# Hybrid attention, RWKV and mixture-of-experts kernel: the steps of iterations 6 to 14 take other slots

## What is computed

```python
x = x + attention(layernorm(x))          # causal, one head, W_Q W_K W_V
x = x + moe(layernorm(x))                # 32 experts of width 64, top 4, plus a shared expert of width 128
x = x + rwkv_block(layernorm(x))         # time mixing (a recurrence over tokens), then channel mixing of width 512
x = x + moe(layernorm(x))                # the same experts again
```

## Time and profile before

| what | value |
|---|---|
| median of 3 runs | 845.95 us (844.31 to 846.03) |
| the profiled execution's own time | 845.29 us |
| its span in the trace | 843.0 us |
| mean granted clock of PE, share of full | 0.998 |
| busy share of PE, DVE, POOL, ACT | 96%, 79%, 71%, 68% |

### The profile page before, as it was taken

How to read it: one execution, slowest core, us unless ns; L and a number is a source line. 1 busy time by engine, 2 the same in 40 slices (tenths; PEclk the granted TensorE clock), 3 DMA queues, 4 the chain that set the end, 5 groups by cost and what they waited for, 6 DMA issues and landing times. The chain is left out here.

```text
span 843.0 us, 12771 instructions
## 1 busy us (share of the span) xinstructions
PE 810.1 (96%) x3876; PEld 607.2 (72%) x3876; DVE 668.9 (79%) x1539; ACT 569.4 (68%) x1033; POOL 597.8 (71%) x470
## 2 busy tenths in 40 slices
PE   7799999999999999999999999999999989999998
PEld 4577878667676676777678776787767757778785
DVE  6776777898898988989786897868977788777765
ACT  3587785877758767679474875748665675677453
POOL 2178778858767678488586876857687684967775
PEclk9999999999999999999999999999999999999999
DMA  9054443334145152550544407443264323526542
GB/s 320 18 126 104 101 97 75 83 76 104 38 103 113 42 126 50 104 126 1 132 89 116 108 16 151 103 108 81 53 136 111 83 63 69 127 50 125 117 115 72
DMA packets 47892, 80.73 MB, mean 96 GB/s; under 512 B 3280, under 2 KB 12624, under 8 KB 47440
## 3 DMA queue, kind: packets, MB, share of 16 engines
q1 hardware_dynamic: 47536, 79.72, 41.0%
q10 hardware_dynamic: 288, 0.20, 0.1%
HBM read 75.19 MB, written 4.72 MB: 95 GB/s over the span
## 5 line engine op out<-in xcount | busy, mean ns | idle before, releaser
L473 POOL TENSOR_TENSOR m_h<-m_v,m_wb 128x512 f32<-128x512 f32 x256 | 344.2, 1355 | 145.1 <-issue 47.1
L563 ACT ACTIVATE m_th<-pa 128x512 f32<-128x512 f32 x240 | 142.6, 596 | 136.4 <-PE pa L827 132.9
L1185 DVE TENSOR_TENSOR m_v<-m_th,pb 128x512 f32<-128x512 f32 x224 | 151.2, 677 | 29.0 <-PE pb L827 11.0
L336 POOL TENSOR_TENSOR m_hl<-m_h,m_hh 128x512 fp32r<-128x512 f32 x85 | 114.8, 1350 | 52.1 <-ACT m_hh L725 51.7
L825 PE MATMUL pa<-m_xh,w1h 128*128 128x512 f32 x272 | 141.7, 521 | 0.3 <-issue 0.3
L725 ACT ACTIVATE m_hh<-m_h 128x512 fp32r<-128x512 f32 x178 | 111.3, 626 | 33.1 <-POOL m_h L473 32.9
L825 PE MATMUL pb<-m_xh,w3h 128*128 128x512 f32 x272 | 117.9, 433 | 5.5 <-DVE m_v L1185 5.4
L336 DVE TENSOR_TENSOR m_hl<-m_h,m_hh 128x512 fp32r<-128x512 f32 x93 | 84.0, 904 | 41.0 <-ACT m_hh L725 41.0
L827 PE MATMUL pb<-m_xh,w3l 128*128 128x512 f32 x272 | 107.9, 397 | 0.0
L826 PE MATMUL pb<-m_xl,w3h 128*128 128x512 f32 x272 | 107.8, 396 | 0.0
L826 PE MATMUL pa<-m_xl,w1h 128*128 128x512 f32 x272 | 107.7, 396 | 0.0
(11 more groups left out here) (259 smaller groups left out, 1640.3 us busy)
## 6 DMA issues: line engine op xcount, KB each, us to landing
m_wb<-w_scratch SPq DMA_DIRECT2D x126, 512.0 KB, 6.7
x_sb<-in_x SPq DMA_DIRECT2D x8, 256.0 KB, 7.2
m_wb<-in_w SPq DMA_DIRECT2D x2, 1024.0 KB, 6.7
x_out<-x_sb SPq DMA_DIRECT2D x7, 256.0 KB, 7.0
...
```

The source lines that it names most:

```text
L336: eng.tensor_tensor(m_hl[:, at, :], hidden(g, p), m_hh[:, at, :].bitcast(F32), ALU.subtract)\
L473: pool.tensor_tensor(hidden(g, p), gated(g, p), m_wb[:, p % (GRING * GP), :], ALU.mult).then_inc(sig["m_h"], 1)
L563: ins = act.activation(m_th[:, p % 2, :], pa[p % 2][:, :], ACT.Silu)
L1185: dve.tensor_tensor(gated(g, p), m_th[:, r, :], pb[r][:, :], ALU.mult).then_inc(sig["m_v"], 1)
```

## The change

Only slot numbers change, for modes 2 to 6 (iterations 6 to 14), on all four compute engines. No operation, wait, tile, transfer or unit comes or goes, and the sets NATIVE and LOW_ON_POOL stay. In each tuple the entries of modes 0, 1 and 7 are the same as before. Lines that only "..." stands for are unchanged; each pair is one step, in the order POOL, ACT, PE, DVE.

The moves that the text below speaks of, slot before and after (the same slot number on two engines is not the same moment):

| engine, line, step | mode 3 (6, 8, 10) | mode 4 (7, 9, 11) | mode 2 (12) |
|---|---|---|---|
| PE L1030, output product of time mixing | 10 to 7 | | 11, same |
| PE L986, expert counts | 47, same | 36 to 37 | 38 to 41 |
| PE L996, transposes of r_w | 48 to 49 | 42, same | 46 to 47 |
| PE L1062, value product | 47 to 50 | 50, same | 50 to 49 |
| PE L1023, receptance | 45, same | | 33 to 37 |
| PE L976, router product | 34 to 32 | 24 to 30 | 23 to 24 |
| ACT L667, L670, exponentials | 45 to 42 | | 33 to 35 |
| ACT L663, t_r | 46 to 43 | | 36, same |
| ACT L660, t_v | 37 to 33 | | 33 to 28 |
| ACT L628, r_wT | 48 to 45 | 42 to 40 | 47 to 43 |
| DVE L1309, L1320, softmax and top 4 | 41, 41 to 34, 39 | 24, 29 to 30, 31 | 27, 36 to 27, 34 |
| DVE L1339 to L1349, r_w and r_carry | 45 to 43 | 34 to 37 | 39 to 37 |
| DVE L1391 to L1399, scans | | 1 to 2 | 44 to 43 |
| DVE L1402, L1405, denominator, numerator | | 1 to 5 | 44 to 43 |
| DVE L1465, reciprocals 0; 1; 2 and 3 | | 33; 41; 40 to 7; 23; 17 | 45; 53; 51 to 44; 51; 50 |
| POOL L498, L500 | 38 to 35 | | 28 to 25 |
| POOL L503, L505 | 39 to 37 | | 33 to 36 |
| POOL L510, input of channel mixing added | 34 to 43 | 40 to 50 | 46 to 40 |

```diff
--- before.py
+++ after.py
...
 def pro_step(q, slot, mode):
-  if slot == (0, 16, 3, 13, 7, 11, 1, 20)[mode]:
+  if slot == (0, 16, 1, 11, 11, 8, 0, 20)[mode]:
...
-  if slot == (15, 24, 17, 30, 41, 43, 37, 28)[mode]:
+  if slot == (15, 24, 17, 29, 43, 40, 36, 28)[mode]:
...
 def time_begin(m, slot, mode):
-  if slot == (3, 0, 2)[mode]:
+  if slot == (3, 1, 2)[mode]:
...
-  if slot == (17, 15, 20)[mode]:
+  if slot == (17, 16, 19)[mode]:
...
-  if slot == (30, 28, 38)[mode]:
+  if slot == (30, 25, 35)[mode]:
...
-  if slot == (33, 33, 39)[mode]:
+  if slot == (33, 36, 37)[mode]:
...
 def channel_step(m, slot, mode):
-  if slot == (46, 34, 40, 40)[mode]:
+  if slot == (40, 43, 50, 35)[mode]:
...
-  if slot == (9, 17, 19, 17)[mode]:
+  if slot == (10, 16, 18, 16)[mode]:
...
-  if slot == (22, 26, 29, 29)[mode]:
+  if slot == (23, 25, 31, 31)[mode]:
...
 def pro_step(q, slot, cmix, mode):
-  if slot == (12, 24, 17, 23, 17, 31, 11, 19)[mode]:
+  if slot == (12, 24, 14, 25, 22, 32, 13, 19)[mode]:
...
-  if slot == (17, 27, 20, 31, 19, 34, 15, 21)[mode]:
+  if slot == (17, 27, 22, 27, 26, 35, 16, 21)[mode]:
...
-  if slot == (18, 27, 26, 35, 24, 38, 19, 24)[mode]:
+  if slot == (18, 27, 26, 33, 30, 38, 19, 24)[mode]:
...
-  if slot == (35, 44, 47, 48, 42, 45, 36, 35)[mode]:
+  if slot == (35, 44, 43, 45, 40, 45, 41, 35)[mode]:
...
 def time_begin(m, slot, q, mode):
-  if slot == (16, 10, 15)[mode]:
+  if slot == (16, 10, 17)[mode]:
...
-  if slot == (19, 17, 20)[mode]:
+  if slot == (19, 16, 20)[mode]:
...
-  if slot == (28, 25, 33)[mode]:
+  if slot == (28, 24, 32)[mode]:
...
-  if slot == (35, 33, 37)[mode]:
+  if slot == (35, 28, 33)[mode]:
...
-  if slot == (37, 36, 46)[mode]:
+  if slot == (37, 36, 43)[mode]:
...
-  if slot == (36, 33, 45)[mode]:
+  if slot == (36, 35, 42)[mode]:
...
 def channel_step(m, slot, mode):
-  if slot == (38, 34, 41, 38)[mode]:
+  if slot == (38, 31, 39, 37)[mode]:
...
-  if slot == (19, 28, 27, 29)[mode]:
+  if slot == (17, 25, 27, 28)[mode]:
...
-  if slot == (28, 30, 31, 31)[mode]:
+  if slot == (28, 26, 35, 35)[mode]:
...
-  if slot == (42, 36, 43, 40)[mode]:
+  if slot == (42, 35, 43, 41)[mode]:
...
-  if slot == (42, 38, 44, 44)[mode]:
+  if slot == (42, 36, 45, 41)[mode]:
...
-  if slot == (42, 40, 47, 44)[mode]:
+  if slot == (42, 38, 45, 41)[mode]:
...
-  if slot == (42, 41, 47, 45)[mode]:
+  if slot == (42, 41, 45, 43)[mode]:
...
-  if slot == (47, 41, 47, 47)[mode]:
+  if slot == (42, 45, 46, 45)[mode]:
...
-      if slot == (10, 10, 10, 9, 8, 10, 11, 11)[it.mode]:
+      if slot == (10, 10, 9, 11, 10, 9, 11, 11)[it.mode]:
...
 def pro_step(q, slot, begin, cmix, mode):
...
-  if slot == (18, 27, 18, 29, 22, 35, 16, 9)[mode]:
+  if slot == (18, 27, 19, 29, 26, 33, 17, 9)[mode]:
...
-  if slot == (20, 29, 23, 34, 24, 38, 19, 17)[mode]:
+  if slot == (20, 29, 24, 32, 30, 37, 19, 17)[mode]:
...
-  if slot == (30, 40, 38, 47, 36, 44, 30, 22)[mode]:
+  if slot == (30, 40, 41, 47, 37, 45, 26, 22)[mode]:
...
-  if slot == (36, 44, 46, 48, 42, 45, 35, 30)[mode]:
+  if slot == (36, 44, 47, 49, 42, 47, 39, 30)[mode]:
...
 def time_begin(m, slot, q, cmix, mode):
-  if slot == (19, 17, 20)[mode]:
+  if slot == (19, 17, 19)[mode]:
...
-  if slot == (31, 24, 34)[mode]:
+  if slot == (31, 24, 32)[mode]:
...
-  if slot == (35, 30, 39)[mode]:
+  if slot == (35, 33, 34)[mode]:
...
-  if slot == (38, 33, 45)[mode]:
+  if slot == (38, 37, 45)[mode]:
...
 def time_out(m, slot, q, mode):
-  if slot == (11, 11, 10, 8)[mode]:
+  if slot == (11, 11, 7, 6)[mode]:
...
 def channel_step(m, slot, q, mode):
-  if slot == (22, 30, 33, 31)[mode]:
+  if slot == (22, 28, 34, 33)[mode]:
...
-  if slot == (43, 39, 43, 42)[mode]:
+  if slot == (45, 35, 45, 42)[mode]:
...
-  if slot == (44, 40, 45, 43)[mode]:
+  if slot == (45, 37, 46, 43)[mode]:
...
-  if slot == (45, 41, 46, 45)[mode]:
+  if slot == (46, 40, 47, 44)[mode]:
...
-  if slot == (46, 42, 47, 45)[mode]:
+  if slot == (46, 44, 47, 46)[mode]:
...
-  if slot == (50, 47, 50, 50)[mode]:
+  if slot == (49, 50, 50, 50)[mode]:
...
-      if slot == (13, 21, 15, 23, 13, 27, 14, 14)[it.mode]:
+      if slot == (13, 21, 13, 25, 12, 30, 13, 14)[it.mode]:
...
 def pro_step(q, slot, cmix, mode):
-  if slot == (1, 16, 2, 15, 5, 9, 2, 22)[mode]:
+  if slot == (1, 16, 0, 11, 10, 9, 0, 22)[mode]:
...
-  if slot == (5, 20, 10, 20, 15, 15, 4, 22)[mode]:
+  if slot == (5, 20, 7, 24, 18, 15, 7, 22)[mode]:
...
-  if slot == (16, 28, 22, 32, 24, 35, 20, 27)[mode]:
+  if slot == (16, 28, 24, 29, 28, 36, 20, 27)[mode]:
...
-  if slot == (18, 28, 27, 41, 24, 35, 20, 28)[mode]:
+  if slot == (18, 28, 27, 34, 30, 37, 20, 28)[mode]:
...
-  if slot == (19, 34, 36, 41, 29, 38, 22, 30)[mode]:
+  if slot == (19, 34, 34, 39, 31, 37, 20, 30)[mode]:
...
-  if slot == (29, 40, 39, 45, 34, 41, 30, 34)[mode]:
+  if slot == (29, 40, 37, 43, 37, 42, 32, 34)[mode]:
...
 def time_begin(m, slot, mode):
-  if slot == (4, 2, 2)[mode]:
+  if slot == (4, 1, 2)[mode]:
...
-  if slot == (10, 7, 10)[mode]:
+  if slot == (10, 7, 12)[mode]:
...
-  if slot == (27, 16, 29)[mode]:
+  if slot == (27, 17, 26)[mode]:
...
-  if slot == (29, 25, 36)[mode]:
+  if slot == (29, 27, 36)[mode]:
...
 def time_finish(m, slot, mode):
-  if slot == (42, 44, 1)[mode]:
+  if slot == (42, 43, 2)[mode]:
...
-  if slot == (44, 44, 1)[mode]:
+  if slot == (44, 43, 5)[mode]:
...
-  if slot == (46, 45, 33)[mode]:
+  if slot == (46, 44, 7)[mode]:
...
-  if slot == (50, 53, 41)[mode]:
+  if slot == (50, 51, 23)[mode]:
...
-  if slot == (49, 51, 40)[mode]:
+  if slot == (49, 50, 17)[mode]:
...
-  if slot == (51, 53, 43)[mode]:
+  if slot == (51, 53, 45)[mode]:
...
-  if slot == (53, 53, 47)[mode]:
+  if slot == (53, 53, 49)[mode]:
...
 def time_out(m, slot, mode):
-  if slot == (7, 9, 10, 13)[mode]:
+  if slot == (7, 11, 8, 10)[mode]:
...
 def channel_step(m, slot, mode):
-  if slot == (42, 34, 37, 34)[mode]:
+  if slot == (40, 28, 39, 36)[mode]:
...
-  if slot == (5, 12, 1, 12)[mode] and m == 0:
+  if slot == (5, 17, 17, 7)[mode] and m == 0:
...
-  if slot == (10, 16, 19, 16)[mode]:
+  if slot == (11, 17, 19, 16)[mode]:
...
-  if slot == (14, 24, 25, 24)[mode]:
+  if slot == (16, 20, 27, 22)[mode]:
...
-  if slot == (33, 31, 35, 31)[mode]:
+  if slot == (31, 26, 37, 33)[mode]:
...
-  if slot == (51, 51, 49, 49)[mode]:
+  if slot == (52, 53, 52, 51)[mode]:
...
-      if slot == (11, 20, 12, 23, 8, 27, 10, 10)[it.mode]:
+      if slot == (11, 20, 16, 25, 13, 29, 11, 10)[it.mode]:
```

## The result

The changed kernel takes 838.14 us (median of 4 runs, 837.64 to 840.14) beside 845.13 of the kernel before (4 runs): a ratio of 0.9922, 95% interval 0.9900 to 0.9943. The forecast was 843.8 with a range of 839.0 to 850.5, so it had the sign and a third of the size, and the time lies under the range. The profiled execution took 837.64, its span 835.9.

A forecast was written before the change was run, and what follows sets the result against it. PE's work was taken as the bound wherever it does not wait; +2.4 - 5.1 + 0 + 0.6 = -2.1 us took the profiled 845.29 to 843.2, 843.8 as median (0.66 higher), range 839.0 to 850.5.

The forecast's parts named there:

- What bounds the kernel: Whole kernel: PE's work bounds it (busy 96%), so the change is worth the PE waits it removes or makes.
- The four kinds of the prediction: PE waits, iterations 6 to 14: r_carry 3.2, DVE's gate 4.0, POOL's low part 1.0, t_v 1.9; given as 10.7 us.
- Part 1: End of iterations 6, 8, 10 (mode 3): value product uncovers a shortened chain, transposes at 48.4; +0.8 each, +2.4 us.
- The bounds: End of iterations 6, 8, 10: from -1.1 an iteration (three: -3.4) to +2.9 (three: +8.7).
- the reasons given: End of 6, 8, 10: earlier softmax, top 4 and exponentials, unit 13's low part after r_w, L510 moved, shorten the chain.
- Part 2: Starts of iterations 7, 9, 11 (mode 4): earlier m_wb and gate 1 remove PE waits; -1.7 each, -5.1 us.
- Part 3: Iterations 12 to 14: in 12 t_v's wait is replaced by a similar later one, 0; 13 and 14 together +0.6.
- A: Ends of 6, 8, 10: value product missed as cover, chain ends nearer 50.5; slower, 850.2 us; chance 0.27.
- B: Iterations 6, 8, 10: the clock falls, 1.7 us each; slower, 848.9 us; chance 0.10.
- C: All waits at the ends go; faster, 838.1 us, or 834.5 if iteration 12 loses its wait too; chance 0.13.

The follow-up runs named there:

- the test with the one entry back: Changed kernel with one entry put back, the copy t_v (L660) in mode 2 on ACT at slot 33 instead of 28: 0.9878, 835.33 us.

## Why the prediction was wrong

**What bounds the kernel**: right in kind. PE's waits in iterations 6 to 14 go from 11.4 to 5.7 us, at the places that the earlier trace rows name; that is about 5.7 of the 7.0. The rest is in the main the clock of iteration 12, 0.97 before and 1.00 here. (The four kinds of the prediction add up to 10.1, not 10.7; the 10.7 has a fifth in it, 0.6 for the normalised tile in iteration 12.)

**Part 1, the step that failed.** "I walked the new order by hand ... the high part of unit 12 (0.6), its low part on DVE beside L505 (until 46.4), gate 14 (0.7), and r_pos, r_w, r_carry (1.3): the transposes can start at 48.4". They start at 46.6. Of the 1.85, 0.63 is ACT (exponentials at 43.67, not 44.3). 0.85 is the low part: I let DVE stand behind L505, but it began 0.09 ahead and took 0.69, so it ends at 44.92; where it begins 0.06 behind, the run with softmax and top 4 back shows 1.77, the length in the earlier trace rows (the walk had left 1.5 for it). Then 0.60 from there to the end of r_carry (44.92 to 46.32, 1.40 instead of 2.0), and this is the same thing again: r_w began 0.28 ahead of POOL's next product and took 0.47. In the kernel before, it began behind one (POOL L473 at 498.61):

```profile
499.43 1.05 DVE L1343 SCALAR_TENSOR_TENSOR r_w<-r_pos,r_ws 128x128 f32<-128x128 f32 x1
```

Of all this, 0.23 is not gained, since PE had not yet come to the transposes. The rest of the part is right: from transposes to end 4.8 was forecast and 4.8 measured (51.4 - 46.6), and the value product does uncover the chain when it moves alone (865 us). I wrote that a walk misses waits and does not invent them; this one had one that did not come. The bounds held: the best end was -1.1 an iteration, measured -0.95 in 8 and 10, and nothing in 6.

What keeps iteration 6 from it is another tie, some 10 us earlier. First iteration 6 (from 348.62), then iteration 8 (from 448.42), of the changed kernel:

```profile
385.24 1.30 POOL L336 TENSOR_TENSOR m_hl<-m_h,m_hh 128x512 fp32r<-128x512 f32 x1 [2.45 <-ACT m_hh L725]
385.25 1.84 DVE L1384 SCALAR_TENSOR_TENSOR t_eb<-t_k,vec,t_h 128x512 f32<-128x512 f32 x1
...
484.96 0.74 DVE L1384 SCALAR_TENSOR_TENSOR t_eb<-t_k,vec,t_h 128x512 f32<-128x512 f32 x1
485.06 1.80 POOL L336 TENSOR_TENSOR m_hl<-m_h,m_hh 128x512 fp32r<-128x512 f32 x1 [2.55 <-ACT m_hh L725]
```

Where DVE is 0.1 ahead, L1384 takes 0.74 and the iteration 51.4. Where POOL is, L1384 takes 1.84, top 4 and gate 13 are later (PE waits 0.43), r_w then begins 0.06 behind a POOL product and takes 1.38 (PE waits 0.44), and the iteration takes 52.3. Ten profiles here have the changed kernel's slots in mode 3. Of their 30 iterations, 11 have L1384 at 1.8 and last 52.3 to 52.4, and 19 have it at 0.74 or 0.75 and last 51.4. Ten of the 11 are iteration 6; the other is iteration 8 of the run with L516 two slots later, so it is not the iteration's place in the loop that decides. So 0.95 of the gain in an iteration depends on a tie that the slots do not settle.

Of the reasons given, the exponentials on ACT were needed (their return, with t_r and r_wT, costs 25 us). That the keys' earlier slots let ACT be early is not shown. L510 and the earlier softmax and top 4 are worth 0.8 to 0.9 an iteration at the end, and by ratio nothing that these runs tell from zero.

**Part 2**: mechanism right, size somewhat high. POOL's first product was forecast near 5.7 and came at 5.8 in iteration 7, whose -1.7 is the forecast; 9 and 11 gain 1.0 and 1.2, since L1460 (1.69 beside POOL's low part) makes gate 0 later there. What the part did not see is how much hung on it: with early m_wb and the old order gate 1 comes at 9.1, and mode 3 alone is slower than before.

**Part 3**: the wait moved from t_v to gate 10, 1.9 to 2.0, as written, and the test with the one entry back proves why. The term was 0 and measured -1.1. The waits of PE in that iteration add up to 3.0 before and 3.5 after (0.6 for f_hn at unit 7 went, 0.9 before L1070 came), so this gain is the clock, which stayed at 1.00 this time. Where it fell in both kernels, in the run with modes 2, 5 and 6 alone, the iteration gained 0.6.

**The rivals.** A is out, since r_carry comes early. B is out here, granted clock 1.00 in all of 6 to 11, though where waits of 3.0 and 1.4 do stand there it falls to 0.50. C, all waits at the ends gone, is what happened, and its 838.1 is the measured time, but partly by chance: its terms were -3.4, -5.1 and +0.6, the measured ones -1.9, -3.9 and -1.2. It had 0.13, too little, because the forecast took one outcome of a near tie between two engines for the only one. And the range began at 839.0, so that it left out both times of C, 838.1 and 834.5, and not only its end, as was written.
